# Decoder layer on one core: mixtures built from a shifted share, layer-norm shifts reduced on VectorE, low-rank stage in token halves

## What is computed

```python
h = layer_norm(x, ln1_w, ln1_b)
hh = time_shift(h)                          # the token before; zero for the first
xk = h * att_tmk + hh * (1 - att_tmk)       # xv, xr likewise
k, v, sr = xk @ Wk.T, xv @ Wv.T, sigmoid(xr @ Wr.T)
x = x + (sr * wkv(time_decay, time_first, k, v)) @ Wo.T
h = layer_norm(x, ln2_w, ln2_b)
hh = time_shift(h)                          # xk, xr with ffn_tmk, ffn_tmr
x = x + sigmoid(xr @ Wrec.T) * (square(relu(xk @ Wkey.T)) @ Wval.T)
# the whole: the block above, attention, a low-rank FFN
x = x + _L0_attn_ref(_layernorm(x), ...)
x = x + _L0_xattn_ref(_layernorm(x), ctx, ctx)     # 16x16 scores per token, over heads
x = x + gelu(_layernorm(x) @ U1 @ V1 + b1) @ U2 @ V2 + b2     # rank 64, 1024 wide
```

## Time and profile before

| | |
|---|---|
| runs | 1202.82, 1202.70, 1201.68 us; median 1202.7 us |
| span of the profiled execution | 1199.4 us |
| outside the span (median less span) | 3.3 us |
| PE busy | 1020.8 us, 85% |
| DVE busy | 952.5 us, 79% |
| ACT busy | 940.2 us, 78% |
| POOL busy | 901.1 us, 75% |
| mean granted TensorE clock | 0.947 of full speed |
| shares of the chain that ended last | PE 46%, ACT 25%, DVE 13%, issue 7%, POOL 6% |

### The profile page before, as it was taken

The page is one execution under the profiler, slowest core; times in us unless marked ns, Lnnn a source line. Parts: engine busy times, 40 slices in busy tenths (PEclk is TensorE's granted clock), DMA queues, the critical chain, the costliest instruction groups (busy, mean ns, idle before and its releaser), DMA issues.

```text
span 1199.4 us, 14602 instructions
## 1 busy us (share of the span) xinstructions
PE 1020.8 (85%) x3584; PEld 586.0 (49%) x3584; DVE 952.5 (79%) x2092; ACT 940.2 (78%) x2007; POOL 901.1 (75%) x862
## 2 busy tenths in 40 slices
PE   2569698989899898989899898989898998969506
PEld 1237264654647363655646373645546473727202
DVE  3654889898989899798979898898979888757470
ACT  3778779888888979888888889888888888584504
POOL 0220997969696988969696978969696969978780
PEclk9889799999999999999999999999999999989767
DMA  5010020201111020201111110202011010201000
GB/s 176 18 23 31 1 53 1 71 0 54 18 54 19 9 62 1 72 0 53 18 53 18 33 38 1 72 0 62 9 53 36 17 37 0 54 1 36 1 17 18
DMA packets 38983, 38.54 MB, mean 32 GB/s; under 512 B 2932, under 2 KB 38648, under 8 KB 38904
## 3 DMA queue, kind: packets, MB, share of 16 engines
q1 hardware_dynamic: 30456, 29.38, 7.4%
q0 software_dynamic: 8448, 8.39, 4.6%
HBM read 29.38 MB, written 8.39 MB: 31 GB/s over the span
## 4 chain that ended last, share of the span: by engine, by line
PE 46%; ACT 25%; DVE 13%; issue 7%; POOL 6%; SPq 1%; DMA 0%; ACTq 0%; POOLq 0%; DVEq 0%
PE bank L832 18%; PE bank L889 12%; PE bank L920 5%; ACT n L480 4%; PE bank L839 4%; DVE bank L1345 4%; POOL prod L329 3%; ACT shift L473 3%; ACT q L480 3%; PE bank L913 3%; PE bank L932 2%; POOL prod L350 2%; DVE stat L1154 2%; ACT hidden L598 1%; ACT rr L546 1%
## 5 line engine op out<-in xcount | busy, mean ns | idle before, releaser
L329 POOL TENSOR_TENSOR prod<-q,kv_ctx 128x256 f32<-128x256 f32 (+5 forms) x448 | 360.1, 853 | 140.6 <-ACT q L480 140.6
L350 POOL TENSOR_TENSOR prod<-prob,v_dh 128x256 f32<-128x256 f32 (+3 forms) x256 | 383.9, 1606 | 0.0
L832 PE MATMUL bank<-xk,w_key 128*128 128x512 f32 x512 | 233.4, 605 | 11.3 <-DVE xk L1196 11.3
L889 PE MATMUL bank<-w_val,hidden 128*128 128x256 f32 x1024 | 225.9, 379 | 0.0
L1345 DVE TENSOR_REDUCE bank<-prod 128x64 f32<-128x256 f32 (+3 forms) x256 | 192.0, 819 | 34.8 <-POOL prod L350 25.4
L889 PEld LDWEIGHTS bank<-w_val,hidden 128*128 128x128 f32 x1024 | 193.5, 190 | 31.7 <-issue 6.7
L1318 DVE TENSOR_REDUCE score<-prod 128x16 f32<-128x256 f32 (+5 forms) x448 | 177.1, 466 | 19.5 <-POOL prod L329 19.4
L832 PEld LDWEIGHTS bank<-xk,w_key 128*128 128x128 f32 x512 | 97.7, 193 | 127.7 <-issue 111.0
L846 PE MATMUL bank<-ident,n 128*128 128x128 f32 x384 | 66.2, 302 | 103.4 <-ACT n L480 101.0
L565 ACT ACTIVATE hidden<-bank 128x512 f32<-128x512 f32 x128 | 74.1, 593 | 82.8 <-PE bank L832 82.7
L846 PEld LDWEIGHTS bank<-ident,n 128*128 128x128 f32 x384 | 49.3, 155 | 159.6 <-issue 153.7
(11 more groups left out here) (95 smaller groups left out, 1909.9 us busy)
## 6 DMA issues: line engine op xcount, KB each, us to landing
x_in<-in_x SPq DMA_DIRECT2D x16, 512.0 KB, 3.5
x<-in_x POOLq DMA_DIRECT2D x16, 512.0 KB, 5.7
kv_ctx<-in_ctx SPq DMA_DIRECT2D x16, 512.0 KB, 4.5
out<-y_out SPq DMA_DIRECT2D x16, 512.0 KB, 3.2
w_key<-in_wkey SPq DMA_DIRECT2D x1, 1024.0 KB
w_val<-in_wval SPq DMA_DIRECT2D x1, 1024.0 KB
w_k<-in_wk SPq DMA_DIRECT2D x1, 256.0 KB, 3.6
w_v<-in_wv SPq DMA_DIRECT2D x1, 256.0 KB, 4.4
```

The source lines that it names most:

```text
L329: ins = pool.tensor_tensor(o, a, b, ALU.mult)
L350: ins = pool.tensor_tensor(o, ph[:, HB * n:HB * n + HB, 0:keys].unsqueeze(2).to_broadcast(shape), vh[:, :, 0:keys].unsqueeze(1).to_broadca ...
L832: mm = pe.matmul(to[:, :], w[:, fi, P * f:P * f + P], src[:, fi, :], start=(fi == 0), stop=(fi == CH - 1))
L889: mm = pe.matmul(bank[6 + t // 2][:, C * (t % 2):C * (t % 2) + C], hidden[:, j, P * t:P * t + P], w_val[:, j, :], start=(j == 0), stop=(j ...
```

## The change

Five edits; the order of stages in every engine's `step` is kept but for the places shown.

1. **Mixtures.** The shares change engines. ACT writes the share of the token before, 2x255 columns, with the norm's bias as bias (L504 of the new kernel). The first columns, which have no token before, are written for both f by one copy from a small constant tile `lone` (L501), so 5 of them a group in place of 10. DVE adds the token's own share over 512 contiguous columns (`add_now`, L1442). Each mixture has its own semaphore, but DVE waits for all shares of an f before its first.
2. **Norm shifts.** `mv` gets a third column that holds -1, ACT writes rstd over the variance (L457), and DVE makes the shift as the product over the three columns (L1400, `tensor_reduce` with mult). `shift_1` to `shift_4` get places in DVE's `step`. The negated mean is gone.
3. **back** is likewise a product of two columns (L1418 on DVE), which ACT prepares in two instructions (`back_ratio`, L473 and L474); L456 and the four L465 are gone.
4. **Low-rank stage in token halves.** U1, V1 and U2 take 256 tokens at a time, the halves in the two column or row halves of the array, so `pT` and `qT` hold 64 ranks of either half on 128 partitions in 256 columns in place of 512. V2 works on 64 rows for either half; its four matmuls and those of b2 now stand together, and `v2_mm` counts once. `gelu` reads its 512 columns from two banks. The keys' matmul j = 0 waits for gelu 6 in place of 5.
5. **Buffers.** `n4` shares `n2`, `last_residual` writes into `x3` in place of `y_out`; the loop runs steps 6 to 13, the rest is unrolled.

```diff
-            def shift_of(n, g):
-                act.wait_ge(nmean_done[n], upto(g, 1))
-                act.wait_ge(rstd_done[n], upto(g, 1))
-                for t in range(TT):
-                    ins = act.activation(shift[n][:, t:t + 1], nmean[n][:, t:t + 1], ACT.Identity,
-                                         scale=rstd[n][:, t:t + 1])
-                ins.then_inc(shift_ready[n], 1)
...
+            def shift_of(n, g):
+                dve.wait_ge(rstd_done[n], upto(g, 1))
+                dve.tensor_reduce(shift[n][:, :], mv[n][:, :, :], AX.X, ALU.mult).then_inc(shift_ready[n], 1)
...
+            def scale_back(g, par):
+                dve.wait_ge(ratio_done, upto(g, 1))
+                if some(g - 1):
+                    dve.wait_ge(x1_done, upto(g - 2, 2))
+                dve.tensor_reduce(back[par][:, :], ratio[par][:, :, :], AX.X, ALU.mult).then_inc(back_done, 1)
...
-                act.activation(out[:, :, 0:1], x[:, :, 0:1], ACT.Identity,
-                               bias=first_b[:, m, f:f + 1], scale=w)
-                return act.activation(out[:, :, 1:T], x[:, :, 1:T], ACT.Identity,
-                                      bias=col(norm + "_b", f), scale=w)
...
+                if f == 0:
+                    act.activation(dst[:, :, :].rearrange("p c (s t) -> p c s t", s=SEQ)[:, :, :, 0],
+                                   lone[:, CH * m:CH * m + CH, :], ACT.Copy)
+                norm = MIXES[m][1]
+                return act.activation(seqs(dst, f)[:, :, 1:T], by_seq(src)[:, :, 0:T - 1], ACT.Identity,
+                                      bias=col(norm + "_b", f), scale=before_w[:, CH * m + f:CH * m + f + 1])
...
+            def add_now(dst, f, src, m):
+                return dve.scalar_tensor_tensor(out=dst[:, f, :], in0=bank[src], scalar=now_w[:, CH * m + f:CH * m + f + 1],
+                                                in1=dst[:, f, :], op0=ALU.mult, op1=ALU.add)
...
+                for fi in range(CH):
+                    for e in range(2):
+                        mm = pe.matmul(bank[U1_BANK][RANK * e:RANK * e + RANK, 0:W // 2], w_u1[:, fi, :],
+                                       n4T[:, fi, W // 2 * e:W // 2 * e + W // 2],
+                                       start=(fi == 0), stop=(fi == CH - 1))
...
+            def project_v2(g):
+                for e in range(2):
+                    r = RANK * e
+                    pe.matmul(bank[Y_BANK[e]], ones[r:r + 1, :], b2_row[r:r + 1, :, :].rearrange("p e c -> p (e c)"),
+                              start=True, stop=False)
+                pe.wait_ge(qT_done, upto(g, 1))
+                for t in range(2):
+                    for e in range(2):
+                        rows = slice(RANK * e, RANK * e + RANK)
+                        mm = pe.matmul(bank[Y_BANK[e]][:, C * t:C * t + C], qT[rows, P * t:P * t + P],
+                                       w_v2[rows, :], start=False, stop=(t == 1))
+                mm.then_inc(v2_mm, 1)
...
             def last_residual(g, par, s):
+                dve.wait_ge(v2_mm, upto(g, 1))
+                dve.wait_ge(n4_done, upto(g, 1))
                 if s == 0 and some(g):
                     dve.wait_ge(out_stored, 16 * g)
-                dve.wait_ge(v2_mm, upto(g, 2, s + 1))
-                dve.tensor_tensor(pair(y_out, s), bank[s][:, :], pair(x3[par], s), ALU.add).then_inc(y_done, 1)
+                dve.tensor_tensor(pair(x3[par], s), bank[Y_BANK[s]], pair(x3[par], s), ALU.add).then_inc(y_done, 1)
```

More of the change, by code:

```diff
@@ L118, in build @@
         n1 = [sb(f"n1_{p}", [P, TT, C]) for p in range(2)]
-        now_w, prev_w, first_b = (sb(n, [P, len(MIXES), CH]) for n in ("now_w", "prev_w", "first_b"))
+        now_w, before_w = (sb(n, [P, len(MIXES) * CH]) for n in ("now_w", "before_w"))
+        lone = sb("lone", [P, len(MIXES) * CH, SEQ])
         xk, xv, xr = (sb(n, [P, CH, W]) for n in ("xk", "xv", "xr"))
@@ L219, in drive @@
         def drive(eng, fill, step, drain, enter=None):
-            for i in range(-2, LOOP[0]):
+            for i in range(-1, LOOP[0]):
                 fill(i, i % 2, lambda lag, i=i: 0 <= i - lag < NG)
@@ L469, in shift_of @@
-            def shift_of(n, g):
-                act.wait_ge(nmean_done[n], upto(g, 1))
-                act.wait_ge(rstd_done[n], upto(g, 1))
-                for t in range(TT):
-                    ins = act.activation(shift[n][:, t:t + 1], nmean[n][:, t:t + 1], ACT.Identity,
-                                         scale=rstd[n][:, t:t + 1])
-                ins.then_inc(shift_ready[n], 1)
+                act.activation(mv[1][:, :, 1], lnc[:, :], ACT.Exp, scale=-0.5).then_inc(rstd_done[1], 1)
@@ L477, in normalise, with back_ratio @@
+            def back_ratio(g, par):
+                act.wait_ge(ln_done[1], upto(g, 1))
+                if some(g - 1):
+                    act.wait_ge(back_done, upto(g - 2, 1))
+                act.activation(ratio[par][:, :, 0], lnc[:, :], ACT.Exp, scale=0.5)
+                act.activation(ratio[par][:, :, 1], lnv[1][:, :], ACT.Exp, scale=-0.5).then_inc(ratio_done, 1)
             def normalise(n, g, dst, src, done):
@@ L480, in normalise @@
                     ins = act.activation(dst[:, t, :], src[:, t, :], ACT.Identity,
-                                         bias=shift[n][:, t:t + 1], scale=rstd[n][:, t:t + 1])
+                                         bias=shift[n][:, t:t + 1], scale=mv[n][:, t, 1:2])
                 ins.then_inc(done, 1)
@@ L509, in att_now, with share_before @@
[L509 to L517 removed]
+            def share_before(dst, f, src, m):
+                if f == 0:
[4 more added lines that the diff above has]
+                                      bias=col(norm + "_b", f), scale=before_w[:, CH * m + f:CH * m + f + 1])
@@ L585, in copy_n4T @@
                 act.wait_ge(tr4_mm, upto(g, 2, f + 1))
-                if f == 0 and some(g):
+                if some(g):
                     act.wait_ge(u1_mm, upto(g - 1, 1))
-                act.activation(n4T[:, f, :], bank[4][:, :], ACT.Copy).then_inc(n4T_done, 1)
+                act.activation(n4T[:, f, :], bank[TR4_BANK[f]], ACT.Copy).then_inc(n4T_done, 1)
             def copy_pT(g):
@@ L592, in copy_pT, with both_halves @@
                 if some(g):
-                    act.wait_ge(v2_mm, upto(g - 1, 2))
-                act.activation(pT[:, :], bank[3][:, :], ACT.Copy).then_inc(pT_done, 1)
+                    act.wait_ge(v1_mm, upto(g - 1, 4))
+                act.activation(pT[:, :], bank[U1_BANK][:, 0:W // 2], ACT.Copy).then_inc(pT_done, 1)
+            def both_halves(j):
+                lo, hi = LOW_BANK[j // 2], HIGH_BANK[j // 2]
+                at = (W // 2) * (j % 2)
+                first = psum[:, lo:lo + 1, at:at + W // 2].to_broadcast([P, 2, W // 2])
+                ap = [list(v) for v in first.ap]
+                ap[1][0] = 512 * (hi - lo)
+                return bass.AP(first.tensor, first.offset, ap)
             def gelu(g, j):
-                act.wait_ge(v1_mm, upto(g, 8, j + 1))
-                act.activation(hidden[:, j, :], bank[HIDDEN_BANKS[j % 4]][:, :], ACT.Gelu_apprx_tanh,
+                act.wait_ge(v1_mm, upto(g, 4, j // 2 + 1))
+                act.activation(seqs(hidden, j), both_halves(j), ACT.Gelu_apprx_tanh,
                                bias=vec[:, B1_AT + j:B1_AT + j + 1]).then_inc(gelu_done, 1)
             def copy_qT(g):
-                act.wait_ge(down_mm, upto(g, 8))
-                act.activation(qT[:, :], bank[4][:, :], ACT.Copy).then_inc(qT_done, 1)
+                act.wait_ge(down_mm, upto(g, 4))
+                if some(g):
+                    act.wait_ge(v2_mm, upto(g - 1, 1))
+                act.activation(qT[:, :], bank[DOWN_BANK][:, 0:W // 2], ACT.Copy).then_inc(qT_done, 1)
             def step(i, p, on):
@@ L1295, in second_residual @@
                 dve.wait_ge(x_added, 16 * (g + 1))
-                dve.scalar_tensor_tensor(out=pair(x2[par], s), in0=bank[6 + s][:, :], scalar=0.5,
+                if some(g - 1):
+                    dve.wait_ge(x3_done, upto(g - 2, 2, s + 1))
+                dve.scalar_tensor_tensor(out=pair(x2[par], s), in0=bank[VAL_BANK[s]], scalar=0.5,
                                          in1=pair(x1[par], s), op0=ALU.mult, op1=ALU.add).then_inc(x2_done, 1)
```

681 lines of the change are left out of this document (460 added, 221 removed).

## The result

The changed kernel takes 1245.41 us (median, 1244.84 to 1246.32) against 1202.76 us before: ratio 1.0355, 95% interval 1.034 to 1.037, so 43 us slower. The profiled execution spans 1244.5 us, against 1199.4. Forecast was slower, 1216 us with a range from 1190 to 1236: the direction held, the size did not.

The account below looks back on a forecast made before the run. Bound: a chain through ACT's list, then PE with DVE as second bound. Full steps +22.8 us (12 x 1.9), ends -10, so +12.8 on the 1199.4 span, 1212.2, plus 3.3 to the median: 1216 us, range 1190 to 1236.

Parts of the forecast that it names:

- What bounds the kernel: Each engine's order decides; the step's chain, 66.8 us, has two parts, with DVE a second bound of the later one.
- Part A: Chain from norm 3's ln on ACT to the first U2 matmul, 21.2 us: 1.0 us a step longer.
- Part B: Chain from first U2 through receptance projection, keys, values and gate_values to norm 3's ln: 0.8 us a step longer.
- The clock: Rival: PE idles more ahead of both r projections, 0.4 to 0.9 us a step, up to 1227; 0.10 of forecast's chance.
- Filling and draining: Ahead of the first q 4 us saved, at the end 6 us saved: -10 us together.
- The prices of small things: Per instruction: DVE reduction 0.15 us alone, 0.1 in a stream; first column on ACT 0.25; mixture additions nothing.
- bare column-half loads: Rival: U2's 16 pairs a step each show 0.14 us of load, +27 us, 1243; chance 0.05, without any overlap 1271, 0.02.
- Rival 1: ACT's list stays the bound, DVE reaching the shifts in time: 1.6 us a step shorter, 1174 us; chance 0.13.

Follow-up runs that it names:

- g4: Changed kernel, all waits kept, with matmuls of no use in all four idle stretches of PE in a step: 1230.63 us, 1.0238 of the kernel before.
- g3: Changed kernel with all of V2 ahead of key j = 1 on PE and the norm shifts at other places of DVE's list: 1177.44 us, 0.9805 of before.
- f2: Changed kernel with the four norm shifts back on ACT at their old places: 1223.78 us, 1.0182 of the kernel before.
- g2: Changed kernel with all of V2 ahead of key j = 1 on PE and the norm shifts back on ACT: 1185.55 us, 0.9866 of the kernel before.
- g1: Changed kernel with all of V2 ahead of key j = 1 on PE, DVE's list as in the change: 1209.33 us, 1.0064 of the kernel before.
- f1: Changed kernel with the first last_residual moved behind mixture r of f = 1 on DVE: 1218.15 us, 1.0137 of the kernel before.

## Why the prediction was wrong in size

**What bounds the kernel** held: the two parts, ACT's list in part A, and DVE as second bound of part B: in the kernel before, its idle time ahead of the first `gate_values` is at most 0.13 us in any of the 12 full steps.

**Part A** held in its mechanism. Said: q 1.3 us later, 2.8 to 3.0 after norm 3's mean, ln to q here 3.04; a wait of DVE at shift 4 of 1.2 and at shift 2 of 0.6, measured 1.31 and 0.60; PE's wait for bb ahead of r of f = 1, there. The sum was too small: said +1.0, measured 22.64 - 21.25 = +1.4 with the clock kept up and +1.64 without. The walk ended 0.4 us early. In the step shown it is 0.1 early at q, 0.2 at the end of bb, 0.3 at U1's start and 0.4 at its end; I put that down to a hop left out at each link, which no run tests.

**Part B**, U2 to receptance: said +0.8, measured 1.05 (g4) to 1.15. I had compared with 619.21, where the chain has the receptance's first row, and not with its start at 619.04: 0.2 of the difference. The wait was said at 1.45 and is 1.64, that at `last_residual` "near 5" and is 4.94.

**The clock** is the step that failed. It stood among the rivals, as 0.4 to 0.9 us a step, 5 to 11 us within the range's upper end, and not in the sum. The rows had r for f = 1 at 2.32 and 1.98, so a fall behind idle time was in sight, and I was adding two idle stretches to each step. It cost 1.24 us a step, 15 us (g4). I had looked for it at the r projections only, and there is a second place, the receptance projection, on the chain itself: 3.75 us for 1.97 in the rows shown, and over 3.2 us in 6 of the 12 full steps.

**Filling and draining** failed too: said -10, measured +2.6 and -2.8, so 10 us off. Two rows of the filling before:

```profile
53.96 5.07 PE L832 MATMUL bank<-xk,w_k 128*128 128x512 f32 x8 [6.99 <-DVE xk L1196]
...
80.82 5.29 PE L832 MATMUL bank<-xk,w_key 128*128 128x512 f32 x8 [4.37 <-DVE xk L1196]
```

and the same two after:

```profile
52.24 6.59 PE L887 MATMUL psum<-xk,w_k 128*128 128x512 f32 x8 [4.67 <-DVE xk L1442]
...
79.37 6.69 PE L887 MATMUL psum<-xk,w_key 128*128 128x512 f32 x8 [3.63 <-DVE xk L1442]
```

The work is there 1.7 and 1.5 us earlier, as saved, and ends at 58.8 and 86.1 as before (59.0 and 86.1): the matmuls start sooner and run slower, at a granted clock of 0.55 in both rows for 0.72 and 0.69 before. No run fills the idle time there, so that the clock took these savings is read from rows, not tested. The first q is 1.4 late by the same wait as in the full steps (2.45 us for its shift). Of the draining only the tail of the last group, 81.6 us from its q for 84.3, gained.

Altogether, on the span: said 22.8 - 10 = 12.8, measured 45.2 - 0.2 = 45.0. The waits under-walked make 7, the clock 15, the ends 10. The 3.3 us between span and median came out as 0.9 (1245.41 less 1244.5), which takes 2.4 off again.

**The prices of small things** held. The reduction takes 0.14 to 0.17 us alone (said 0.15), two in a stream 0.23; a lone copy 0.10 in a stream (its row is 0.22 long, the next starts 0.10 later). Five of them stand for ten first columns. The mixtures' additions cost nothing more. The rival of **bare column-half loads** fell: 16 records of U2 take 1.95 us where 8 of twice the width took 1.94, so there is no room for 0.14 us of bare load in each of 8 pairs. "TensorE: Matmul & The Clock Gate" of the Trainium skill, section "The mechanism", which lets a load overlap only where row groups differ, isn't borne out by that row. **Rival 1** (ACT's list stays the bound) fell as the profile had spoken: DVE was not at shift 3 in time. g3 shows what it would have been worth with DVE's list in another order.

## What to carry to other kernels

An instruction moved to another engine costs its place in that engine's list, both ways: what it waits for, and what is queued behind its wait. Four shifts a step, each 0.15 us of DVE in place of 0.95 of ACT, lost 2 us a step at one set of places (the change beside f2) and gained 0.5 at another a few lines away (g3 beside g2). Where a change adds idle time on PE, put the clock into the sum and ask which matmuls come right behind it; and where matmuls are put together, ask who reads their bank and what overwrites it next.

## What the hardware did that I had not expected

The clock's fall can be moved: filler in two of four idle stretches raised the mean clock of the full steps from 0.95 to 0.98 and gained nothing, since it now fell where part A waits for r; filler in all four gained 15 us. How long the clock is low doesn't give its price either: g1 has it lower in its full steps than f1 (mean 0.96, f1 0.97) and is 9 us faster. Its r of f = 0 runs at 3.4 to 3.8 us in place of 1.98 in every full step, which costs part A 0.3 (22.94 for 22.64 in g4), while its receptance projection keeps its 1.89. And earlier work in the filling bought nothing where PE came out of idle time: 1.7 us earlier, 1.5 us slower.
